# Two decoder stages cut into halves of the tokens, and a third stage threaded between their pieces

## The reference, cut to what matters

```
x = norm(x + L0_attn(x))           # "self attention", stage A below
x = norm(x + L0_xattn(x, ctx, ctx))# "context attention", stage C
x = norm(x + L0_ffn(x))            # "first experts", stage X

# L0_attn: 8 sequences of 256 tokens, causal within each
q, k, v = x @ Wq, x @ Wk, x @ Wv               # 16 query heads on 8 key heads, 128 wide
a = tril((q k^T / sqrt(128)) ** 2 * exp(logG[t] - logG[s]))
y = (a v) / (sum(a) + 1e-6);  out = y @ Wc + bc
# L0_xattn: per batch of 256 tokens, 16 heads of 32: causal softmax(q ctx^T / sqrt(32)) ctx
# L0_ffn: 128 router logits, top 4; mix of 8 basis blocks of 256: silu(gate_k) * up_k,
#   weighted by the token's coefficients, @ w_down; plus a shared expert of width 512
```

## Time and profile before

| | |
|---|---|
| median of 3 runs | 2399.05 us (2389.92 to 2410.53) |
| span of the profiled execution | 2397.8 us |
| busy, share of the span | PE 89%, PEld 71%, DVE 53%, ACT 41%, POOL 29% |
| the costliest groups | L1136 (tiles of X) 602 us, L307 (projections of A) 457 us of busy PE |

### The profile page before, as it was taken

How to read it: one execution, slowest core, us unless ns; L and a number is a source line. 1 busy time by engine, 2 the same in 40 slices (tenths; PEclk the granted TensorE clock), 3 DMA queues, 4 the chain that set the end, 5 groups by cost and what they waited for, 6 DMA issues and landing times.

```text
span 2397.8 us, 37028 instructions
## 1 busy us (share of the span) xinstructions
PE 2137.6 (89%) x13669; PEld 1705.2 (71%) x13669; DVE 1263.5 (53%) x3237; ACT 993.1 (41%) x2275; POOL 689.1 (29%) x633
## 2 busy tenths in 40 slices
PE   7899999999997898788999999978999868888774
PEld 6789889889885666577888888865656356666542
DVE  2654554553557666554111123346777676777556
ACT  3322322332324766432211211235566647777632
POOL 2832332332331111103443410044454331322110
PEclk9999999999997866599999999989999889999986
DMA  3210110100001110101010000024233310000001
GB/s 140 86 41 22 34 40 17 38 28 26 28 13 54 36 37 10 41 18 36 27 53 18 18 27 1 1 40 63 49 55 56 99 41 25 17 19 6 1 10 71
DMA packets 41730, 86.45 MB, mean 36 GB/s; under 512 B 6224, under 2 KB 20816, under 8 KB 38736
## 3 DMA queue, kind: packets, MB, share of 16 engines
q1 hardware_dynamic: 41552, 84.08, 12.6%
HBM read 63.55 MB, written 4.26 MB: 28 GB/s over the span
## 4 chain that ended last, share of the span: by engine, by line
PE 39%; issue 14%; DVE 8%; ACT 5%; POOL 3%; DMA 1%; SPq 0%; DVEq 0%; ACTq 0%; POOLq 0%
PE PS L1136 14%; PE PS L1208 4%; PE PS L1235 3%; PE PS L1619 3%; PE PS L1715 3%; DVE aM L1852 2%; ACT xP L2377 1%; PE PS L1683 1%; DVE st L137 1%; PE PS L2229 1%; POOL xN L1021 1%; PE PS L1670 1%; PE PS L1703 1%; DVE PS L2499 1%; PE PS L1726 1%
## 5 line engine op out<-in xcount | busy, mean ns | idle before, releaser
L1136 PE MATMUL PS<-WH,bXH 128*128 128x512 f32 x512 | 201.0, 392 | 5.4 <-POOL WL L1429 5.4
L1136 PE MATMUL PS<-WL,bXH 128*128 128x512 f32 x512 | 200.4, 391 | 0.0
L1136 PE MATMUL PS<-WH,bXL 128*128 128x512 f32 x512 | 200.3, 391 | 0.0
L1339 DVE SCALAR_TENSOR_TENSOR s<-s,cf,PS 128x256 f32<-128x256 f32 x112 | 53.9, 481 | 249.0 <-ACT s L1254 240.0
L1852 DVE TENSOR_REDUCE aM<-PS 128x4 f32<-128x1024 f32 x128 | 153.8, 1222 | 57.9 <-PE PS L1683 56.9
L1254 ACT ACTIVATE s<-PS 128x256 f32<-128x256 f32 x128 | 49.3, 385 | 278.7 <-PE PS L1136 278.5
L307 PE MATMUL PS<-aXH,QKH 128*128 128x512 f32 x384 | 154.0, 401 | 0.0
L307 PE MATMUL PS<-aXH,QKL 128*128 128x512 f32 x384 | 151.6, 395 | 0.0
L307 PE MATMUL PS<-aXL,QKH 128*128 128x512 f32 x384 | 151.5, 395 | 0.0
L1791 ACT ACTIVATE aPT<-PS 128x1024 f32<-128x1024 f32 x128 | 128.4, 1024 | 49.6 <-PE PS L1703 48.8
L506 ACT ACTIVATE sq<-PS 128x768 f32<-128x768 f32 x64 | 52.0, 813 | 210.1 <-PE PS L397 163.5
(11 more groups left out here) (406 smaller groups left out, 6112.6 us busy)
## 6 DMA issues: line engine op xcount, KB each, us to landing
lgB<-gate_sums SPq DMA_DIRECT2D x32, 256.0 KB, 3.6
sg<-in_gu SPq DMA_DIRECT2D x8, 1024.0 KB, 4.8
aqs<-aQH SPq DMA_DIRECT2D x64, 128.0 KB, 4.1
gQK<-in_Wqk SPq DMA_DIRECT2D x8, 768.0 KB, 5.9
xN<-in_xT SPq DMA_DIRECT2D x4, 1024.0 KB, 10.4
gC<-in_Wc SPq DMA_DIRECT2D x8, 512.0 KB, 4.5
xN<-in_x SPq DMA_DIRECT2D x4, 1024.0 KB, 7.2
cst<-in_cT SPq DMA_DIRECT2D x8, 512.0 KB, 4.7
```

What stands on the lines that cost most here:

```text
L1136: mm = e.matmul(PS[:, b, :], x[:, kc, 128 * t:128 * t + 128], w[:, kc, :], start=kc == 0 and i == 0, stop=kc == KC - 1 and i == 2)
```

## The change

Each of A, C and X becomes a `Stage` whose engine functions are generators that stop at numbered ticks, and `decoder` interleaves the ticks of the three by one list, `order`, the same on every engine and for the giving out of banks.

- **A in halves of the tokens**: key heads 0 to 7 for the first 1024 tokens (steps 0 to 15), then again for the others. The arithmetic on PE is the same; the weights of a key head are loaded and split twice (16 times instead of 8 for q/k and for the output, 7 times instead of 4 for the values). From step 17 on A uses banks 0 to 3 alone.
- **C** as ticks, 20 to a batch (5 for four heads), all buffers single, banks 4 and 5 for scores, 6 and 7 for everything else; all copies of transposed weights on ACT. Batches 0 to 3 stand beside A's steps 17 to 31, batches 4 to 7 beside X's tiles 0 to 49, three tiles for four heads. It waits for the first half of A alone (`first_half`), and lies in the SBUF that the first half's tokens held.
- **X in halves of the tokens**: per half 80 tiles of 128 tokens by one block (the shared expert is blocks 0 and 1, the basis blocks follow); every weight is loaded and split twice. The down projection is done in three parts, after blocks 0, 1 and 9, two or three ticks behind the tile. The router's steps are spread over the first tiles of a half. In the first half silu is made as 0.5 * g * (1 + tanh(g/2)), with one DVE operation more per tile. Up to tick 75 X uses banks 0 to 3 alone.
- The norm after A for tokens 0 to 1023 comes during steps 16 to 18; norms have two sets of small tiles (`Space`).
- `attention1` stages its weights at an address of their own and doesn't wait for X before loading and splitting them; its first two token splits on ACT wait for all 11 weight splits on POOL.

```diff
-    def take(self, key, n=1, pack=False):
-        starts = [s for s in range(0, 8, n) if not any(self.held[s:s + n])]
+    def take(self, key, n=1, pack=False, among=(0, 8)):
+        starts = [s for s in range(among[0], among[1], n) if not any(self.held[s:s + n])]
...
+def in_order(order, pieces):
+    for s, n in order:
+        for _ in range(n):
+            next(pieces[s])
...
-def attention0(K):
+def attention0(K, alone):
...
-    steps = [(g, p) for g in range(8) for p in range(NP)]
+    steps = [(g, 2 * h + p) for h in (0, 1) for g in range(8) for p in (0, 1)]
+    events = {0: 0, 4: 1, 8: 2, 12: 3, 20: 4, 24: 5, 28: 6}
...
+    for p, n in enumerate((16, 17, 32, 33)):
+        norm_at.update({(n, 6): ("stats", p), (n, 7): ("seed", p), (n + 1, 0): ("newton", p), (n + 1, 1): ("apply", p)})
...
+            among = (0, 8 if n < alone else 4)
...
         for n in range(N + 2):
-            if n < N:
-                project(n)
...
+            for m in range(3):
+                if n < N:
+                    project(n, m)
...
+                yield
+            for i in (0, 1):
+                if 2 <= n:
+                    out(n - 2, 2 * i)
+                    out(n - 2, 2 * i + 1)
+                yield
             if 1 <= n <= N:
                 attend(n - 1)
+            if n and n in events:
+                values(events[n])
+            yield
             if n < N:
                 scores(n)
+            yield
             if 1 <= n <= N:
                 turn(n - 1)
+            yield
...
+        norms[NP - 1].apply_act(e)
...
+    starts = [20 * j + 12 * (j // 4) for j in range(J)]
+    first, last = -12, starts[-1] + 28
...
+    score_at, flip_at = {0: 0, 3: 1, 5: 2, 8: 3, 10: 4, 13: 5, 15: 6, 18: 7}, {2: 0, 4: 1, 7: 2, 9: 3, 12: 4, 14: 5, 17: 6, 19: 7}
+    turn_lags, context_lags = (-4, 1), (-11, -1)
...
+            if r in score_at:
+                R.use(("c_s", j, score_at[r]), 2, s_exp.upto(8 * j + score_at[r] + 1), among=(4, 6))
+            elif r in flip_at:
+                R.use(("flip", j, flip_at[r]), 2, f_out.upto(8 * j + flip_at[r] + 1), among=(6, 8))
...
+def experts0(K, apart):
...
+    U, first, last = 160, -6, 163
+    outs = [(80 * h + 8 * k + i, 80 * h + 8 * k + i + (3 if k == 9 else 2), i, c, z)
+            for h in (0, 1) for z, (k, c) in enumerate(((0, 2), (1, 4), (9, 0))) for i in range(8)]
...
+    turn_at = {-2: 0, -1: 1, 76: 2, 80: 3}
...
+    for p in range(NP - 1):
+        n = 79 + 80 * (p // 2) + 4 * (p % 2)
+        norm_at.update({n: ("stats", p), n + 1: ("newton", p), n + 2: ("apply", p)})
...
+            if by_tanh(u):
+                step(e.scalar_tensor_tensor(out=s1[z][:, :], in0=s1[z][:, :], scalar=1.0, in1=gate, op0=ALU.add, op1=ALU.mult))
...
+        for tick in range(first, last):
+            if tick == -2:
+                for x in old:
+                    e.wait_ge(*x)
+            if 0 <= tick < U:
+                tile(tick)
+            for v in out_at.get(tick, ()):
+                out(v)
+            for v in flip_at.get(tick, ()):
+                flip(v)
+            if tick in turn_at:
+                turn(turn_at[tick])
...
-    wst = PT[:, :, :, :].rearrange("p a b c -> p (a b c)")[:, 512:3584].rearrange("p (k n) -> p k n", k=4)
+    wst = nc.alloc_sbuf_tensor_at("awst", [128, KC, 768], F32, offset=K.floor + 24576)
...
                 if bt >= 2:
                     e.wait_ge(*q_mm.upto(4 * bt - 4))
+                else:
+                    e.wait_ge(*w_lo.upto(11))
...
+def beside(order, s, pieces, t, groups):
+
+    groups, since = list(groups), 0
+    for ticks, units in pieces:
+        order.append((s, ticks))
+        since += units
+        while groups and since >= groups[0][1]:
+            order.append((t, groups[0][0]))
+            since = 0
+            del groups[0]
+    return groups
...
-        stages = [stage(K) for stage in (constants, attention0, cross0, experts0, attention1, cross1, experts1)]
+        first = whole(constants(K))
+        a0 = attention0(K, 17)
+        c0 = cross0(K)
+        e0 = experts0(K, 76)
...
+        A, C, X = 1, 2, 3
+        step = [(1, 3), (1, 3), (1, 3), (1, 3), (1, 3), (1, 3), (1, 2), (1, 1)]
+        pair = [(2, 8), (1, 5), (2, 3)]
+        order = [(0, 1), (A, 1 + 8 * 17 + 4), (C, 11)]
+        late = beside(order, A, step[4:] + 14 * step + [(5, 6), (1, 3), (2, 1)], C, 16 * pair + 3 * [(3, 3)])
+        order += [(X, 1), (A, 5), (X, 3), (A, 5)]
+        order += [(C, n) for n, _ in late]
+        order += [(X, 2)]
+        late = beside(order, X, 76 * [(1, 3)], C, [(3, 3)] + 16 * [(2, 3), (1, 3), (2, 3)] + 9 * [(1, 3)])
+        order += [(C, n) for n, _ in late]
+        order += [(X, 163 - 76)]
+        order += [(i, 1) for i in range(4, 7)]
```

More of the change, by code:

```diff
@@ L289, in attention0 @@
[L289 to L309 removed]
+        p = t // 4
@@ new lines, in tensor, with project @@
+    def tensor(e):
+        def project(n, m):
+            g, p = steps[n]
+            b, left = rooms["qk", n, m]
+            for w in left:
+                e.wait_ge(*w)
+            if m == 0:
+                e.wait_ge(*qk_hi.upto(n // 2 + 1))
+                e.wait_ge(*qk_lo.upto(n // 2 + 1))
+            c = 512 * (p % 2)
+            for kc in range(KC):
+                for i, (w, x) in enumerate(pair3((QKH, XH[p // 2]), (QKL, XL[p // 2]))):
+                    mm = e.matmul(PS[:, b, :], w[:, kc, 128 * m:128 * m + 128], x[:, kc, c:c + 512],
+                                  start=kc == 0 and i == 0, stop=kc == KC - 1 and i == 2)
+            mm.then_inc(qk_mm.sem, 1)
@@ L571, in attended, with norm @@
                                 ALU.mult).then_inc(y_out.sem, 1)
+        def norm(n, k):
+            if (n, k) in norm_at:
+                what, p = norm_at[n, k]
+                if what == "stats":
+                    norms[p].stats(e, step)
+                elif what == "seed":
+                    norms[p].seed(e, step)
+                elif what == "newton":
+                    norms[p].newton(e, step)
+                    norms[p].hand_over(e)
         for n in range(N + 2):
-            if n < N:
-                if n:
-                    e.wait_ge(*s_mm.upto(2 * n))
-                for m in range(3):
+            for m in range(3):
+                if n < N:
+                    if n and m == 0:
+                        e.wait_ge(*s_mm.upto(2 * n))
                     e.wait_ge(*q_hi.upto(3 * n + m + 1))
@@ L601, in vector @@
                     at.then_inc(s_at.sem, 1)
+            norm(n, 6)
+            yield
             if 1 <= n <= N:
@@ L609, in vector @@
                                     ALU.subtract).then_inc(t_lo.sem, 1)
-            if 2 <= n and 28 <= n - 2 < N - 1:
-                norms[n - 30].all_dve(e, step)
-        norms[NP - 1].stats(e, step)
+            norm(n, 7)
+            yield
+        norm(N + 2, 0)
+        yield
+        yield
     def gpsimd(e):
@@ new lines, in tensor @@
+        for tick in range(first, last):
+            j, r = batch(tick, 6)
+            if r >= 0 and r % 5 == 0:
+                attend(j, r // 5)
+            j, r = batch(tick)
+            if r in score_at:
+                scores(j, score_at[r])
+            elif r in flip_at:
+                flip(j, flip_at[r])
+            j, r = batch(tick, 23)
+            if r == 0:
+                finish(j)
+            for i, lag in enumerate(turn_lags):
+                j, r = batch(tick, lag)
+                if r == 0:
+                    turn(j, i)
+            yield
@@ L1358, in vector, with gate @@
+        def gate(p, part):
+            w, rz = pr[p % 2], rzz[:, p % 2, :, :]
+            if part == 0:
                 e.wait_ge(*c_exp.upto(p + 1))
@@ new lines, in gpsimd @@
+    def gpsimd(e):
+        for tick in range(first, last):
+            if tick == -2:
+                for x in old:
+                    e.wait_ge(*x)
+            if 0 <= tick < U and parts(tick)[1] > 2:
+                h, k, i = parts(tick)
+                e.wait_ge(*(t_mul.upto(tick + 1) if k == 3 else t_add.upto(added(tick - 8))))
+                e.wait_ge(*t_mul.upto(tick + 1))
+                e.tensor_tensor(mixed[:, i, :], mixed[:, i, :], s2[tick % 2][:, :], ALU.add).then_inc(t_add.sem, 1)
+            if tick in split_at:
+                w = split_at[tick]
+                e.wait_ge(*w_hi.upto(w + 1))
+                e.tensor_tensor(WL[w % 2][:, :, :], sg[:, :, :], WH[w % 2][:, :, :].bitcast(F32),
+                                ALU.subtract).then_inc(w_lo.sem, 1)
+            if tick in down_at:
+                k, c = down_at[tick], (2, 4, 0)[down_at[tick]]
+                e.wait_ge(*d_hi.upto(k + 1))
+                e.tensor_tensor(DL[:, c:c + 2, :], dst[:, :, :], DH[:, c:c + 2, :].bitcast(F32),
+                                ALU.subtract).then_inc(d_lo.sem, 1)
+            yield
@@ L1478, in attention1 @@
+    K.late, K.loadable, K.projected = norms[NP - 1], K.cross_ends, ()
```

(2 more changed lines are left out.)

1780 lines of the change are left out of this document (898 added, 882 removed).

## The result

The changed kernel takes **2375.3 us** (median of 4 runs, 2370.3 to 2379.5) against 2402.8 for the kernel before in the same comparison: ratio 0.989, 95% interval 0.985 to 0.994. The forecast was 2350, 2.0% less; measured are 1.1%. The direction and the whole range (2300 to 2425) held; the gain is about half of the forecast, and the measured time lies 0.3 us above the forecast case's own range (2315 to 2375). The profiled execution, the longest of the four, has a span of 2377.1, so 28.3 more than the sum of 2348.8.

A forecast was written before the change was run, and what follows sets the result against it. PE was taken as full in A and X's tiles, slow in C and X's start. 755.6 + 77 + 30 + 17 + 524 + 77 + 28 + 27.5 + 812.7 = 2348.8, with 1.25 for the median 2350 us; range 2300 to 2425.

The forecast's parts named there:

- 6 for the norms that DVE now does there: Stage A beside C: DVE's added norms were priced at 6 us of stall.
- A's stall term of 30: Stage A: 1.6 us of stall in each of 15 steps, 24, plus 6 for norms.
- the second rival: ACT's and DVE's in-order queues make PE wait 2.4 us at each of 64 head pairs; 2375 to 2470 us; chance 0.25.
- SP issues the loads ... so I cost it at nothing: Loads of A behind waits for C's values or keys are needed two steps later, so they cost nothing.
- Up to A's step 16 nothing should move: Sign: stage A's steps before C joins it should keep their times.
- The banks, 24: A on four banks instead of eight: 1.2 us stall plus 0.4 for score banks, in each of 15 steps.
- the first rival: C's groups fill the gaps, so the stalls of A and X mostly vanish; 2285 to 2315 us; chance 0.15.
- C's price of 19.2 a batch: PE time of C's pieces at full clock; eight batches 154 us, 77 beside A and 77 beside X.
- stalls of 25 to 85 in place of 58: Stalls of A (30) and X (28) varied to give the forecast case's own range, 2315 to 2375 us.
- the third rival: C's transposes and small matmuls hold PE's clock down inside A and X too; 2400 to 2500 us; chance 0.10.
- the two hand-overs: PE idle from A to X, 17 us, and from X's last tile to attention 1's first projection, 27.5 us.
- X with C: X's stretch with half of C beside it: 524 of X's work, 77 of C, 28 of stalls, 629 us.

The follow-up runs named there:

- run 6: Against the changed kernel, A's norm of tokens 512-1023 starts two thirds of a step later and is dealt out over a whole step: 2359.8 us.
- run 4: Against the changed kernel, the two norms of tokens 0 to 1023 after context attention, beside A in steps 25 and 31, left out: 2358.3 us.
- run 2: Against the changed kernel, SP issues A's loads of query-key, output and value weights one step earlier in its order: 2368.5 us.
- run 3: Against the changed kernel, POOL adds the output bias to the residual one step later at A's start: 2367.5 us.
- run 1: Against the changed kernel, context attention of batches 0-3 stands behind A instead of inside its second half: 2475.8 us.
- run 8: Changed kernel with four repairs: earlier loads, later residual bias, C's norms dealt out, A's second norm later: 2343.7 us.
- run 5: Against the changed kernel, C's first norm beside A dealt out over fourteen ticks, the second moved behind A's step 31; all work kept: 2364.3 us.
- run 12: Against run 10, A's last norm dealt out after X's pieces 6, 10, 14 and 18 instead of in one block: 2332.5 us.
- run 10: Against run 8, X's first four ticks moved ahead of A's last norm on all queues: 2345.0 us.
- runs 7 and 9: Fourteen matmuls on constants ahead of each of A's last two sets of outputs, added to the changed kernel (2362.5 us) and to run 8 (2341.6 us).

## Why the prediction was wrong, point by point

- **The step that failed: "6 for the norms that DVE now does there", inside A's stall term of 30.** These norms cost some 24: 11 in steps 18 and 19 (run 6), some 13 in step 25 and the last stretch (run 4). I priced DVE's work by the row. What counted was that a norm is one block in a queue: the minima, A's additions or ACT's scaling wait behind it, PE waits for them, and the clock falls. The mechanism is the second rival's, in-order queues, but at four places instead of at each pair of heads; at ordinary pairs PE had no wait for C's exponentials.
- **"SP issues the loads ... so I cost it at nothing".** 7.2 in step 21 (run 2). I had named the right row of loads, and said that A's projection would wait if the two steps of cover went. The cover was there for the load's use by PE, but ACT's split of the weights stood in the step of the load itself, with C's copies behind it: the waiter was ACT.
- **"Up to A's step 16 nothing should move".** 4.6 (run 3). POOL's 192 busy of 600 us was an average over a stage; at A's start POOL's timeline has almost no gap, and there the second split now falls two steps earlier.
- **The banks, 24.** 1.24 a step when nothing stands beside A (run 1), so the size was about right. In the changed kernel 12.8 of it is left as waits for the square: C's groups fill a part of it, not most, as the first rival would have it.
- **C's price of 19.2 a batch.** Steps 23 and 29 (26.08 and 26.07, no idle) give 6.6 for three scores, three transposes and one product with the values, where the pieces sum to 5.9: 1.12 times the price, about 86 in place of 77 for half of C.
- **The sum.** The four places cost 11 + 13 + 7.2 + 4.6 = 36, where the forecast had 6: 30 more. C's price adds 9. What is left of the 142, 142 - 36 - 86 = 20, stands against the 24 for the banks: 4 less. That makes the 35, but the 20 is a remainder: the trace names 12.8 of it as waits for the square, and the rest is not shown. Run 8 took back 30 of the 35, 2.6 of them in the matmuls behind A's last two waits. In the working of the forecast itself, stalls of 25 to 85 in place of 58 give 2317 to 2377, not 2315 to 2375, and the 5.87 of A's end stand ahead of the output before the last; the last one waits 1.86 in the kernel before.
- **The clock.** It stood at 0.95 between 410 and 898, at the limit that I had set for being wrong. It is not the third rival: step 23, with 18 transposes and 52 small matmuls of C in it, ran at 1.00, and with the waits repaired the whole stretch stood at 0.98 (run 8). The low windows stand behind waits. By the Trainium skill, "TensorE: Matmul & The Clock Gate", section "PE-mode transpose", the clock gate doesn't open for transposes as for other matmuls; step 23 shows that transposes among A's matmuls don't close it either.
- **Right**: the two hand-overs (16.6 and 24.7 against 17 and 27.5). **Right in part by luck**: X with C (622 against 629). There the forecast had 20 too much for stalls and 13 too little for work: PE is busy for 614.4 of the 622.0, where 524 + 77 = 601 were priced, and 7.6 were idle, where 28 were; in X the first rival was right about the stalls. No table load stands between tanh and the exponentials: the listing of ACT's instructions from 914 to 1200 has none, and the 41 us that I kept for it in the range weren't needed. The Trainium skill, "ScalarE: Activation LUTs", section on table sets, has both in one set, and the trace agrees.

What stays open: why the clock fell in one run and not in another behind the same wait at A's end, and where the part of the remainder lies that is no wait for the square.

## What to carry to other kernels

When two stages share in-order queues, price each block that stays in one piece (a norm, a weight split, a load behind another stage's wait) by what stands behind it on its queue, not by its duration or its engine's mean busy share. Deal such blocks out, or move them to where nothing waits: with the same work run 5 brought A's end 10 us forward, run 6 took 11 out of two steps, and run 12 took 9 out of the hand-over and X together. A saving at a hand-over is only one when the next stage's first stretch is as long as before (run 10 against run 12).

## What the runs showed of the hardware

- A wait of PE of 3.3 us at A's end was followed by 24 matmuls in 8.03 us in the changed kernel and in 5.30 in run 6, by the same instructions behind the same wait. A busy PE (runs 7 and 9) kept 5.3 each time.
- C alone in its new form (run 1) was granted 0.51 over 214 us, nearly the lower level throughout; the old form had 0.70.
- A small DVE operation on 128 x 4 numbers took 1.70 us (at 858.03) where the same operation took 0.17 in A's last norm; POOL was in a subtraction of 2.34 us then, from 857.36 on. Why it took longer is open: no run here varies what stands beside it.
